# A gated linear attention and FP4 feed-forward layer: short rows of small matmuls between long ones, and output projection and two units moved ahead of the key products

## The reference

```
xn = layernorm(x)
q, k, v, g_out = xn @ qk_w.T, xn @ vg_w.T         # 16 heads, DK 16, DV 32
q, k, v = causal conv over 4 positions, then silu; q, k l2-normalised, q scaled
beta = 2 * sigmoid(xn @ b_w.T + biases);  g = -exp(A_log) * softplus(xn @ a_w.T + dt_bias)
for each position t:                               # gated delta rule
    S = S * exp(g_t);  delta = (v_t - k_t S) * beta_t
    S = S + k_t (x) delta;  o_t = q_t S
o = rmsnorm(o) * silu(g_out);  attention = o @ o_w.T
gate, up = xn @ W_gu.T                             # FP4 weights, 1408 + 1408 columns, scales per group of 128
y = (silu(gate) * up) @ W_down.T;  ffn = y / rms(y)
out = x + attention + ffn
```

## Time and profile before

| | |
|---|---|
| median of 3 runs | 3956.02 us |
| lowest, highest | 3924.19, 3962.34 us |
| profiled execution | 3955.46 us |
| its span (first to last instruction) | 3953.7 us |
| mean granted TensorE clock | 0.903 of full |
| PE, DVE, ACT, POOL busy | 87, 61, 45, 33% of the span |

### The profile page before, as it was taken

The page is one execution under the profiler, slowest core; times in us unless marked ns, Lnnn a source line. Parts: engine busy times, 40 slices in busy tenths (PEclk is TensorE's granted clock), DMA queues, the critical chain, the costliest instruction groups (busy, mean ns, idle before and its releaser), DMA issues.

```text
span 3953.7 us, 125312 instructions
## 1 busy us (share of the span) xinstructions
PE 3459.4 (87%) x49728; PEld 2542.6 (64%) x49728; DVE 2399.4 (61%) x5664; ACT 1772.7 (45%) x3595; POOL 1315.6 (33%) x2257
## 2 busy tenths in 40 slices
PE   4888989998889888888988898988989889988896
PEld 3666666666666666666666666666666666666664
DVE  6665656656566656566665666665665656666563
ACT  4444444444444444544444544444444444444452
POOL 2443223433224432234332244321343323443223
PEclk8899898899899988999998999988889998898897
DMA  2111011110111110111101011101111010111110
GB/s 97 31 39 36 26 29 29 39 39 25 37 26 31 39 39 23 29 28 39 39 23 39 25 33 39 39 23 29 28 39 39 23 29 29 39 39 28 34 23 28
DMA packets 318377, 133.06 MB, mean 34 GB/s; under 512 B 277088, under 2 KB 278880, under 8 KB 317792
## 3 DMA queue, kind: packets, MB, share of 16 engines
q1 hardware_dynamic: 313824, 119.26, 11.6%
q10 hardware_dynamic: 4096, 6.42, 0.5%
HBM read 75.30 MB, written 50.33 MB: 32 GB/s over the span
## 4 chain that ended last, share of the span: by engine, by line
PE 67%; DVE 13%; issue 10%; ACT 7%; POOL 2%; DMA 1%; ACTq 0%; DVEq 0%; SPq 0%; POOLq 0%
PE PS L1015 12%; PE PS L975 10%; PE PS L1002 9%; PE PS L1003 7%; PE PS L1196 5%; DVE arena L757 4%; PE PS L1178 3%; PE PS L1057 3%; PE PS L1119 3%; PE PS L1095 2%; DVE arena L876 2%; PE PS L1023 2%; PE PS L1104 2%; DVE qkv L741 2%; PE PS L1043 1%
## 5 line engine op out<-in xcount | busy, mean ns | idle before, releaser
L757 DVE SCALAR_TENSOR_TENSOR arena<-PS,sc,arena 128x256 f32<-128x256 f32 x2112 | 1009.4, 483 | 548.8 <-ACT arena L518 432.7
L448 POOL TENSOR_TENSOR work<-arena 128x31 f32<-128x31 f32 (+15 forms) x992 | 509.7, 514 | 1969.7 <-DMA arena<-scr_a 1894.4
L1002 PE MATMUL PS<-xh,wgu 128*128 128x256 f32 x2816 | 952.2, 366 | 65.2 <-DVE arena L757 39.2
L1003 PE MATMUL PS<-xl,wgu 128*128 128x256 f32 x2816 | 780.3, 305 | 0.0
L1002 PEld LDWEIGHTS PS<-xh,wgu 128*128 128x128 f32 x2816 | 595.7, 212 | 184.7 <-issue 100.3
L1015 PE MATMUL PS<-wdn,inner 128*128 128x512 f32 x1408 | 668.5, 597 | 20.8 <-DVE inner L769 20.8
L518 ACT ACTIVATE arena<-PS,sc 128x256 f32<-128x256 f32 x704 | 334.0, 474 | 765.4 <-PE PS L1003 760.8
L1003 PEld LDWEIGHTS PS<-xl,wgu 128*128 128x128 f32 x2816 | 603.6, 214 | 68.9 <-issue 68.9
L452 POOL TENSOR_TENSOR arena<-arena,work 128x31 f32<-128x31 f32 (+15 forms) x992 | 546.4, 551 | 77.8
L975 PE MATMUL PS<-xnT,wqkv 128*128 128x256 f32 x2048 | 503.2, 398 | 68.6 <-issue 55.8
L975 PEld LDWEIGHTS PS<-xnT,wqkv 128*128 128x128 f32 x2048 | 390.2, 197 | 148.5 <-issue 80.7
(11 more groups left out here) (139 smaller groups left out, 4391.9 us busy)
## 6 DMA issues: line engine op xcount, KB each, us to landing
xt<-in_x SPq DMA_DIRECT2D x64, 256.0 KB, 2.8
scr_a<-arena SPq DMA_DIRECT2D x64, 256.0 KB, 2.0
arena<-scr_a SPq DMA_DIRECT2D x256, 64.0 KB, 3.1
obuf<-in_x SPq DMA_DIRECT2D x64, 256.0 KB, 2.8
scr_t<-arena SPq DMA_DIRECT2D x32, 512.0 KB, 3.2
arena<-scr_t SPq DMA_DIRECT2D x256, 64.0 KB, 2.4
out<-obuf SPq DMA_DIRECT2D x64, 256.0 KB, 2.1
wqkv<-in_wqkv ACTq DMA_DIRECT2D x1, 2048.0 KB, 12.9
```

The lines of the kernel that those rows point to most:

```text
L448: eng.tensor_tensor(pr, la[:, j, j + 1:].unsqueeze(1).broadcast_to([P, w, r]), bc(lt[:, 0:w, j], r), ALU.mult).then_inc(solve_part.sem, 1)
L757: eng.scalar_tensor_tensor(out=fa[:, u % 4, :], in0=PS[:, bank(u, k // 2), k % 2 * NB * P:][:, 0:NB * P], scalar=sc[:, u % 2, KB * m + k:K ...
L1002: eng.matmul(o, w, xh[:, k, :], start=True, stop=False)
L1003: ins = eng.matmul(o, w, xl[:, k, :], start=False, stop=True)
```

## The change

- **X rows and P times u rows.** Each batch's row is cut in two, so there are four rows of 32 matmuls (64 records). Projections 5, 6 and 7 stand between the X rows. Decay matmuls, sums and the turned q and k stand between the P times u rows.
- **Units.** Unit 0 moves ahead of the turning of Y, so the chunk loop holds units 1 to 4 in place of 0 to 3. Units 5 and 6 and the gate projection fill the time before the scaled keys are ready. On DVE, convolution 6 and unit 0 stand before the first `state`.
- **Output.** The turning of o moves ahead of the keys, and the output projection is cut in two halves per batch, each before half a row of key products. On DVE the scaling of o by `ro` stands before the scaled keys, and unit 6 and `hidden(2)` stand before both `a_done`.
- **Banks.** The gate projection goes to banks 2 and 3, the output projection to banks 4 and 5, and `U_PAIRED` falls from 10 to 8.

The diff, cut to its core:

```diff
-U_PAIRED = 10
+U_PAIRED = 8
...
-            project(6)
+            unit(0)
...
-                unit(c)
+                unit(c + 1)
...
+            unit(5)
...
+            unit(6)
+            if n:
...
+            gate(2)
+            eng.wait_ge(*taps_done.at(n, NQKV))
+            eng.activation(qkv[:, 4:NQKV, :], qkv[:, 4:NQKV, :], ACT.Silu).then_inc(silu_done.sem, 1)
             unit(7)
...
+            conv(6)
+            if n:
+                eng.tensor_copy(halo[:, :, :, :], cin[:, :, :, P:]).then_inc(halo_out.sem, 1)
+            unit(0)
...
-                unit(c)
-                if c >= 2:
-                    hidden(c - 2)
+                unit(c + 1)
+                if c in (1, 3):
...
+            unit(5)
+            if t:
+                eng.wait_ge(*ro_done.at(t, 2))
+                eng.wait_ge(*o_gated.at(t, NB))
+                for b in range(NB):
+                    oh = sq[:, b, :].rearrange("p (h v) -> p h v", v=DV)
+                    eng.tensor_tensor(oh, oh, bc(ro[:, b, :], DV), ALU.mult).then_inc(o_scaled.sem, 1)
...
+            unit(6)
+            hidden(2)
+            if n:
+                for b in range(NB):
...
-                    eng.wait_ge(*gs_done.at(n, fill + 1))
-                elif u == 11 and t:
+                elif u == 5:
+                    eng.wait_ge(*decay_done.at(n, 1 if fill else 2))
+                elif u == 7 and t:
                     eng.wait_ge(*attn_added.at(t, fill + 1))
-                elif u != 11:
+                elif u != U_PAIRED + 1:
...
-            for b in range(NB):
+            for q in range(4):
                 if t:
-                    for h in range(H):
+                    b = q // 2
+                    for h in range(q % 2 * HG, (q % 2 + 1) * HG):
                         f, r, e = h // HG, h % HG // 2, h % 2
                         for c in range(NC):
                             s = slice(c * CH, (c + 1) * CH)
                             ins = eng.matmul(x_rows(c, r)[:, 0:3, (b * NHALF + f) * 2 + e, :], tT[s, b, h, :], R[s, b, h, :],
                                              start=(b + f + e == 0), stop=False, skip_group_check=True)
-                    if b == NB - 1:
+                    if q == 3:
                         ins.then_inc(x_out.sem, 1)
-                project(5 + b)
+                if q < 3:
+                    project(5 + q)
+            unit(0)
             if t:
                 for b in range(NB):
                     eng.wait_ge(*y_copied.at(t, b + 1))
...
+            def p_times_u(q):
+                if not t:
+                    return
+                b = q // 2
+                for h in range(q % 2 * HG, (q % 2 + 1) * HG):
+                    f, r, e = h // HG, h % HG // 2, h % 2
+                    for c in range(NC):
+                        s = slice(c * CH, (c + 1) * CH)
+                        ins = eng.matmul(paired(1, b)[s, f, r, e * DV:(e + 1) * DV], D[s, b, h, :],
+                                         u[b][s, r, :, f, e, :], start=False, stop=True,
+                                         skip_group_check=True)
+                if q == 3:
+                    ins.then_inc(pu_out.sem, 1)
+
+            def to_wo(b, part):
+
+                if not t:
+                    return
+                eng.wait_ge(*ot_copied.at(t, b + 1))
+                if n and part == 0:
+                    eng.wait_ge(*(fa_done if b else fa_second).at(n, 7))
+                for kb in (2 * part, 2 * part + 1):
+                    ins = eng.matmul(PS[:, 4 + b, :], oT[b][:, kb, :], wo[:, kb, :], start=(kb == 0),
+                                     stop=(kb == KB - 1))
+                if part:
+                    ins.then_inc(wo_out.sem, 1)
+
+            def turn_o():
+                if not t:
+                    return
+                for b in range(NB):
...
+            def gate(b):
+                if t:
+                    eng.wait_ge(*o_gated.at(t, NB))
+                elif b == 0:
+                    eng.wait_ge(wg_loaded.sem, 16)
+                    eng.wait_ge(wo_loaded.sem, 16)
+                for kb in range(KB):
+                    ins = eng.matmul(PS[:, 2 + b, :], xnT[:, kb, b * P:(b + 1) * P], wg[:, kb, :], start=(kb == 0),
+                                     stop=(kb == KB - 1))
+                ins.then_inc(gate_out.sem, 1)
+
...
+            p_times_u(0)
+            if n:
+                log_decay(0)
+            p_times_u(1)
...
+            p_times_u(2)
+            if n:
+                log_decay(1)
                 eng.wait_ge(*silu_done.at(n, NC))
                 turn_qk(0)
+            p_times_u(3)
+            if n:
                 eng.wait_ge(*ex_done.at(n, 1))
                 turn_qk(1)
-                if not t:
...
+                unit(5)
+                gate(0)
+                unit(6)
+                gate(1)
+            turn_o()
+            for b in range(NB):
...
-                    unit(4 + b)
+                to_wo(b, 0)
+                if n:
                     hold(eng, *knq_copied.at(n, 2 * (b + 1)))
                     hold(eng, *kbq_copied.at(n, 2 * (b + 1)))
-                    if b:
+                    if b == 0:
+                        hold(eng, *gs_done.at(n, NB))
+                    else:
                         hold(eng, *p_done.at(n, b))
...
+                    gram(b, 0)
+                to_wo(b, 1)
                 if n:
...
+                    gram(b, 1)
...
+            unit(7)
+            eng.wait_ge(*p_done.at(n, NB))
```

More of the change, by code:

```diff
@@ L549, in act_step @@
                 eng.activation(lnz[:, :, :], ee[:, :, 0:H], ACT.Ln, bias=1.0).then_inc(lnz_done.sem, 1)
-            for m in range(2, 6):
+            for m in range(2, NQKV):
                 project(m)
@@ L624, in act_step @@
                         eng.wait_ge(*o_gated.at(t, NB))
-                    eng.activation(gs[:, b, :], PS[:, 4 + b, :], ACT.Silu).then_inc(gs_done.sem, 1)
-                for b in range(NB):
-                    eng.wait_ge(*kqn_turned.at(n, b + 1))
-                    if b:
[L629 to L636, removed]
-                                   ACT.Copy).then_inc(kbq_copied.sem, 1)
-                    if t:
-                        eng.wait_ge(*qs_out.at(t, 1))
-                    eng.activation(qtT[:, b, :, :].rearrange("p f t -> p (f t)"), PS[:, 7, NHALF * P:2 * NHALF * P],
-                                   ACT.Copy).then_inc(kbq_copied.sem, 1)
-                    unit(4 + b)
-                unit(6)
-                gate(2)
+                    eng.activation(gs[:, b, :], PS[:, 2 + b, :], ACT.Silu).then_inc(gs_done.sem, 1)
             if t:
@@ L656, in act_step @@
                                ACT.Copy).then_inc(v_copied.sem, 1)
+            gate(3)
             for m in range(4, FM):
@@ L918, in dve_step @@
                 return
+            unit(7)
+            hidden(3)
+            unit(8)
             unit(9)
@@ L1069, in pe_step @@
                     ins.then_inc(y_turned.sem, 1)
-            project(7)
             for c in range(NC):
@@ new lines, in gram @@
+            def gram(b, f):
+                for c in range(NC):
+                    s = slice(c * CH, (c + 1) * CH)
+                    for e in range(2):
+                        for q in range(4):
+                            r = slice(q * 32, (q + 1) * 32)
+                            o = PS[s, q, 0:8 * CH].rearrange("p (w n i) -> p w n i", w=2, i=CH)[:, :, 2 * f + e, :]
+                            ins = eng.matmul(o, kbT[r, f, s], knq[r, f, e, :, s], start=True, stop=True,
+                                             skip_group_check=True)
+                if f == NHALF - 1:
+                    ins.then_inc(gram_out.sem, 1)
@@ L1200, in pe_step @@
                 return
+            unit(7)
+            eng.wait_ge(*p_done.at(n, NB))
             for b in range(NB):
-                if not t:
-                    eng.wait_ge(*p_done.at(n, NB))
                 eng.wait_ge(*silu_done.at(n, NC + 1))
```

115 lines of the change are left out of this document (30 added, 85 removed).

## The result

| | before | after |
|---|---|---|
| median | 3945.44 us (4 runs) | 4065.01 us (4 runs) |
| lowest, highest | 3924.19, 3962.34 | 4045.89, 4083.77 |
| ratio | | 1.0306, 95% interval 1.0228 to 1.0383 |
| profiled execution, span | 3955.46, 3953.7 | 4073.08, 4071.3 |
| mean granted TensorE clock | 0.903 | 0.922 |

The ratios leave out one execution each of e7 (3948.64 us, granted clock 0.817), of e12 (12419.54 us) and of the kernel before beside e5 to e8 (4378.78 us), which ran in a slower state.

A forecast was written before the change was run, and what follows sets the result against it. PE looked like the bound, but POOL's loop holds one stretch at 56.5 us; with 68.5 for the other, a tile takes 125.0, 4.1 more. Over 31 intervals 127, plus some 2, on 3955.5: 4085 us, range 3970 to 4180.

The forecast's parts named there:

- B: Stretch from L904 of b = 1 to the next X rows: POOL's loop holds it at 56.5 us, from 59.3.
- The new waits: PE waits in the stretch from X rows to L904: `ex`, `o_gated`, `p_done`, put at 5.8 us together with unit 4's.
- `ex`: Second half of turned q and k: PE waits about 2.5 us, as ACT's work stands behind the later `pu_out`.
- `p_done`: Half row of b = 1's key products: PE idles about 2 us, as `gate(2)` and `hidden(2)` precede L906 and L908.
- unit 4 and `o_gated`: First decay waits for unit 4 on DVE, to offset 31.1; gate projection waits for `o_gated`, to about 42.8.
- `attn_added`: Before unit 7: PE waits for this DVE signal, so its wait before the X rows is about 5 us, not 7.
- The refills: Three PE issue stops are instruction refills that small matmuls outrun; 3.9 us a tile taken off, 121 us more by the skill's rule.
- The entry of A: X rows to first chunks: projection 7, convolution 6 and unit 0 moved forward; costed at 0, between -1.5 and +1.6 us.
- The clock's cost: Lower granted clock after PE's wait before the X rows: 1.7 us, plus 0.5 for the projections between them.
- A's 68.5: Stretch from X rows to L904 of b = 1: grows from 60.5 to 66.3, plus 1.7 and 0.5 us for the clock.
- step 4 and 5: Key products of b = 0, then b = 1, with halves of output projection (1.8) and half rows (0.8): ends at 66.3.
- The first tile: Start of the run: its L906 comes some 2 us later than before the change.

The follow-up runs named there:

- e7: Changed kernel with the edits of e1 and e2, and batch 1's output projection behind the key products, in stretch B: 3853.15 us, 0.9703 of the kernel before.
- e12: e7 with projections 5 and 6 ahead of PE's wait for tT and only projection 7 between the X rows: 3841.87 us, 0.9713 of the kernel before.
- e5: Kernel before the change, with POOL's inversion shortened (steps 10 to 17 on one row only): 3983.42 us, 1.0066 of the kernel before.
- e8: Kernel before the change, with only the P times u rows cut in quarters, fillers between them: 4002.98 us, 1.0113 of the kernel before.
- e4: Changed kernel with POOL's inversion shortened (steps 10 to 17 on one row only): 4016.14 us, 1.0200 of the kernel before.
- e1: Changed kernel with the last two quarters of P times u together, ahead of the second decay and turned q and k: 3992.68 us, 1.0149 of the kernel before.
- e2: Changed kernel with hidden(2) on DVE behind both L906/L908 pairs, as before the change: 3985.01 us, 1.0146 of the kernel before.
- e9: Kernel before the change, with only unit 6 moved between the two halves of b = 1's key products: 3968.20 us, 1.0023 of the kernel before.
- e3: Changed kernel with all four halves of the output projection behind both key products, in stretch B: 4056.06 us, 1.0328 of the kernel before.
- e11: e7 with P times u back in two rows of 128 records around the first decay: 3870.94 us, 0.9787 of the kernel before.
- e10: The same kernel as e7, measured a second time and profiled: 3848.65 us, 0.9736 of the kernel before.

## Why the prediction was right, and where it was not

**The bound.** The reading that B can't go far below 56.5 us held in the mean, 55.99, with PE waiting for tT in 25 of the 31 tiles. In these the loop took 55.5: 8.6 from L906 to POOL, 37.9 on POOL, 9.0 to the X rows. The 56.5, read from one tile, was 1 too high, and B was not 56 to 57 in every tile: it ran from 54.6 to 58.3. e4 and e5 show that POOL's loop held B after the change and not before.

**The new waits.** All of them were found from the order lists and the durations before, at their places. `ex` was put at 2.5 us and took 2.3; `p_done` at about 2 and took 1.93; unit 4 and `o_gated` were inside the offsets, at 1.1 and 1.2, and took 0.7 and 0.8 in the mean. The prediction calls the four 5.8 us together; its own offsets make 6.8, and 5.8 is the three without unit 4's. Measured are 181 us in 31 tiles, which is 5.8 for all four, so that agreement is chance. e1 and e2 took away the two large ones and each gave its time back. X rows waited 2.5 us in the mean of 24 tiles (83.7 less 8.3 in the first and 14.6 in the last) instead of 5; the wait for `attn_added` was 3.0, and I had it only in a parenthesis.

**The refills.** Of the three stops two went, as worked out, and the one in the chunk loop stayed (one chunk later). The rule of the Trainium skill, "Runtime: NRT & Kernel Launch", section "Instruction fetch mechanics", that crossing a block is mostly hidden, would have left 121 us in the sum; the runs do not bear it out for rows of 32x32 matmuls. Cutting a row took the stops away in e8 and shortened them in e9, and longer rows brought them back in e3, e11 and e12. The trace agrees with the rule for long matmuls: within the loop's rows of these, both kernels show hardly any issue stop (L975's, 55.8 and 52.1 us in the run, stand at the first matmul of a pass of the loop, 29 times).

**The entry of A** was costed at 0 (between -1.5 and +1.6), and its two parts were each larger than that range. The first chunk starts 11.43 us after the X rows instead of 9.17, since projection 7 and unit 0 now stand before it on PE. The four chunks then take 17.9 instead of 21.3. So P times u starts 1.2 us earlier in the mean (29.28 against 30.45). I had taken the middle tile's 29.3 as its start, which agrees with the new mean by luck.

Two things made the chunks shorter. Convolution 6 (2.71 us in the middle tile) no longer stands between the first two `state` on DVE. And the clock was higher. The mean granted clock of the four chunks was 0.70 before, with some of it low in every tile, and 0.87 after. A stretch of each middle tile, before and then after:

```profile
1985.50:1995.60 10.10, 8.39 (x184) 7.13 (x184) 6.87 (x21) 4.00 (x9) 0.00 (x0) 0.50 0.01 2
...
2046.00:2065.00 19.00, 15.73 (x483) 12.30 (x481) 14.35 (x43) 11.11 (x22) 2.25 (x4) 0.91 0.01 3
```

In the changed kernel the chunks took 15.97 us in the 7 tiles where the clock held and 18.4 in the other 24. The prediction read no clock for this part of the kernel before. What part of the 3.4 us is the order's and what the clock's, no run separates.

**The clock's cost** was near in sum and wrong in place. I put 1.7 us behind the wait for tT. There the chunk loop starts 11.02 us after the X rows where the clock held (24 tiles) and 12.85 where it fell (7): 0.4 us in the mean. The sign "the clock should be low right after the X rows start" failed in those 24. The rest came at the gate projection, behind the 2.3 us wait for `ex`:

```profile
2065.00:2075.00 10.00, 6.70 (x216) 4.81 (x217) 2.55 (x6) 2.42 (x6) 0.00 (x0) 1.00 0.01 3
2075.00:2084.00 9.00, 8.38 (x25) 4.67 (x25) 7.39 (x21) 6.40 (x12) 0.00 (x0) 0.62 0.01 2
```

From the first gate half to the second took 5.38 us in the mean, against 4.48 where the clock held: 0.9 us a tile.

**A's 68.5 against 68.44** is closer than its terms deserve. The forecast had P times u start at 31.0 (29.3 and the 1.7 of the clock) and 37.5 us from there to L906. Measured are 29.28 and 39.16. The first part was 1.7 us too long and the second 1.7 too short: the gate projection's 0.9, and the rows and halves of step 4 and 5, put at 0.8 and 1.8, which take about 0.9 and 1.9 to 2.0 each. That the two errors cancel is luck. In single tiles A was 63.8 to 74.4 us, and in 23 of 31 within the 66 to 70 of the prediction.

**The first tile** was put at 2 us and took 10.4. In the other runs it took 2.5 to 11.7 more than before, and 5.4 in e4, which is the same kernel up to that point, so this part is not explained.

**The size.** 4.1 us a tile was forecast and 3.5 measured, 127 and 109 us over the run; the first tile's extra 8 us hid half of the difference. By the ratio 1.0306 the profiled 3955.5 would be 4077.

## What to carry to other kernels

Divide the loop at the points where other engines hand over to PE, and compare each stretch with the loop of the other engines that it can't beat; work may move only into the stretch that has idle time *after* such a move, and here, taking 9.5 us out of a stretch with 3.8 to give won 3.8 and cost 7.3 in the other. Before reordering, list for each signal what newly stands ahead of it on its own engine: one 0.42 us instruction ahead of a signal cost 2.7 us a tile, and the last quarter of a row behind its fillers cost 2.45, 0.9 of it through the clock. The idea of the change was sound: with those two put right and half of the output projection moved back, the same kernel is 2.6 to 3% faster than before instead of 3% slower.

## What the runs showed of the hardware

- Rows of 32x32 matmuls of 128 records can stop for 1.1 to 2.8 us. Rows of 64 with about 1 us of long matmuls between them hardly do (3.8 us in P times u over the run after the cut, 48.6 before). Not every long row stops: e1's did not (4.3 us), e11's did (43.2).
- The stops stand at fixed places, counted in PE's matmul records from the start of a pass of the loop (1554 records). In the kernel before they are at 458 in 30 tiles, at 831 or 958 in 39 cases and at 1336 in 30; in e12 27 stand at 336. From 458 to 582 (where most of the changed kernel's stops in the chunk loop stand) and from 831 to 958 it is 124 and 127 records, which with their weight loads make about 256 instructions. Whatever matmul stands there is the one that waits: a small one mostly, in e12 the first long one behind the row (1.84 us). The first matmul of a pass waits 1.9 us in the mean, 29 times (55.8 us before).
- The mean granted clock rose (0.903 to 0.922, 0.942 in e10's profile) while the kernels got slower and then faster: in these runs it does not follow speed.
- The length of a wait does not alone tell what the clock does behind it. In the changed kernel the granted clock of the X rows' first 4 us was 1.00 behind all waits of up to 2.76 us and 0.50 to 0.67 behind all but one from 3.19 to 8.28 us (1.00 behind 3.31). In e1 it was 0.61 to 0.63 behind five waits of 1.77 to 1.91 us and 1.00 behind one of 3.10.
